# Mixture-of-experts stage: token rows turned by DMA instead of TensorE, weights in a ring of three slots addressed by registers

## The reference

```python
x = x + ga * attn(layernorm(x) * (1 + ca) + sa)        # 16 batches of 512 tokens, width 256
h = layernorm(x) * (1 + cb) + sb
normed = layernorm(h) * rn_g + rn_b
top_w, top_idx = top_k(normed @ router_w.T + router_b, 2)   # softmax over the two
for e in range(8):
    t = layernorm(h) * ln_g[e] + ln_b[e]
    t = gelu(t @ w1[e] + b1[e]) @ w2[e] + b2[e]         # 256 -> 1024 -> 256
    out += combine[e] * t                               # zero unless e is one of the token's two
x = x + gb * out
```

## Time and profile before

| | |
|---|---|
| median of 3 runs | 1253.28 us (1248.76 to 1253.87) |
| the profiled execution | 1263.39 us, span 1261.6 us |
| TensorE busy | 1123.1 us (89%) |
| VectorE busy | 912.2 us (72%) |
| ScalarE busy | 554.1 us (44%) |
| GpSimd busy | 588.1 us (47%) |
| granted TensorE clock, mean | 0.909 |

### The profile page before, as it was taken

How to read it: one execution, slowest core, us unless ns; L and a number is a source line. 1 busy time by engine, 2 the same in 40 slices (tenths; PEclk the granted TensorE clock), 3 DMA queues, 4 the chain that set the end, 5 groups by cost and what they waited for, 6 DMA issues and landing times.

```text
span 1261.6 us, 29766 instructions
## 1 busy us (share of the span) xinstructions
PE 1123.1 (89%) x8408; PEld 892.3 (71%) x8408; DVE 912.2 (72%) x2923; ACT 554.1 (44%) x1098; POOL 588.1 (47%) x487
## 2 busy tenths in 40 slices
PE   5789799889884329999999999999999999999996
PEld 1334454554443318998999999998999999998995
DVE  5577878877886426777777777777777777777775
ACT  1567565666563203433444444433434444433442
POOL 2111554554556572455554454445554444445553
PEclk8788878877796558999999999999999999999998
DMA  5346546556454265877444747457444444445743
GB/s 159 126 155 210 175 154 230 194 179 229 153 179 141 75 217 166 213 208 179 87 84 85 215 90 213 85 128 176 88 84 86 85 85 82 85 87 116 192 83 45
DMA packets 105765, 177.38 MB, mean 141 GB/s; under 512 B 23580, under 2 KB 76968, under 8 KB 99592
## 3 DMA queue, kind: packets, MB, share of 16 engines
q1 hardware_dynamic: 71560, 120.34, 30.7%
q0 software_dynamic: 34176, 56.72, 23.2%
HBM read 228.66 MB, written 63.69 MB: 232 GB/s over the span
## 4 chain that ended last, share of the span: by engine, by line
PE 71%; DVE 9%; issue 4%; POOL 3%; DMA 2%; another core or an unknown queue 1%; ACT 1%; DVEq 1%; POOLq 0%; SPq 0%; ACTq 0%
PE banks L1227 29%; PE banks L1215 29%; PE banks L1180 3%; PE banks L1204 3%; PE banks L1189 3%; DVE st L670 2%; POOL lists L461 2%; DMA lists<-nrm,slot 2%; PE banks L1101 2%; PE banks L1118 2%; DVE rowbuf L788 1%; DVE rowbuf L790 1%; DVE mv L675 1%; DVE resid L844 1%
## 5 line engine op out<-in xcount | busy, mean ns | idle before, releaser
L1215 PE MATMUL banks<-nh,wbuf 128*128 128x256 bf16 x2272 | 467.9, 274 | 9.8 <-ACT gf L641 8.3
L1227 PE MATMUL banks<-wbuf,resid 128*128 128x256 bf16 x3408 | 465.7, 273 | 0.0
L641 ACT ACTIVATE gf<-banks,b1t 128x256 f32<-128x256 f32 x568 | 269.3, 474 | 428.3 <-PE banks L1215 348.8
L497 POOL DMA_INDIRECT out<-rowbuf,ydst x142 | 232.0, 1634 | 353.2 <-DVE rowbuf L1008 279.5
L1227 PEld LDWEIGHTS banks<-wbuf,resid 128*128 128x128 bf16 x3408 | 334.1, 98 | 39.2
L1215 PE MATMUL banks<-nl,wbuf 128*128 128x256 bf16 x1136 | 311.1, 274 | 0.0
L1016 DVE CAST resid<-gf 128x256 bf16<-128x256 f32 x568 | 180.0, 317 | 178.6 <-ACT gf L641 110.9
L1018 DVE TENSOR_TENSOR resid<-gf,resid 128x256 bf16<-128x256 f32 x568 | 241.9, 426 | 19.5
L1215 PEld LDWEIGHTS banks<-nh,wbuf 128*128 128x128 bf16 x2272 | 223.2, 98 | 37.4 <-ACT gf L641 9.7
L461 POOL DMA_INDIRECT lists<-nrm,slot x128 | 138.4, 1081 | 142.2 <-DVE nrm L904 107.6
L488 POOL DMA_INDIRECT resid<-y_rows,ygb x142 | 145.3, 1023 | 54.9 <-issue 43.7
(11 more groups left out here) (184 smaller groups left out, 1101.5 us busy)
## 6 DMA issues: line engine op xcount, KB each, us to landing
wbuf<-wsplit SPq DMA_DIRECT2D x142, 1024.0 KB
rowbuf<-lists SPq DMA_DIRECT2D x71, 264.0 KB
wbuf<-in_L_ffn_w SPq DMA_DIRECT2D x16, 1024.0 KB, 6.7
wsplit<-wbuf SPq DMA_DIRECT2D x16, 1024.0 KB, 5.3
b2t<-in_L_ffn_b SPq DMA_DIRECT2D x71, 128.0 KB
resid<-in_L_attn_x SPq DMA_DIRECT2D x16, 512.0 KB, 7.4
out<-resid SPq DMA_DIRECT2D x16, 512.0 KB
csB<-mod_rows SPq DMA_DIRECT2D x16, 256.0 KB
```

Source lines behind the costliest of these rows:

```text
L497: g.indirect_dma_start(out_rows, bass.IndirectOffsetOnAxis(ap=ydst[:, r, h:h + 1], axis=0), yt[:, r, h, :], None, compute_op=ALU.add).then ...
L641: a.activation(gf[:, c % 2, :], MM[c % 2][:, 0:TOK], ACT.Gelu, bias=b1t[:, r, c:c + 1]).then_inc(gf_s, 1)
L1215: last = t.matmul(MM[c % 2][:, 0:TOK], w, m[:, r, k, :], start=n == 0, stop=n == 5)
L1227: last = t.matmul(ACC[r][h][:, 0:D], g[:, c, h * P:(h + 1) * P], w, start=c == 0 and n == 0, stop=c == NI - 1 and n == 2)
```

## The change

- The transposes of `turn` are gone from TensorE. ScalarE now copies the rows as bf16 straight from `xin` into `xhl`, VectorE writes the rest beside it, and SyncE turns both with two DMA transposes of 128x512 bf16 for a tile (`flip`) into `nhl`. ScalarE and VectorE do this two tiles ahead at chunk 5, SyncE a tile ahead.
- The weights lie in a ring of three slots (`wring`; the third lies over the last batches of `store`, the former `resid`). The two first experts are loaded before the table exists; from then on, when a tile is the first of expert e, expert e + 2 is loaded into the slot that is free (`weights_ahead`). Before, each expert was loaded into both buffers.
- The slot is a number in the table. TensorE reads the slots for two tiles with one load of three registers (`sets_from`), and its matmuls take the address of the weights from a register.
- The biases are now loaded on a condition too. SyncE reads six table entries for a tile, not three.
- VectorE keeps the token numbers in `ytok`, one small copy more for a tile, and builds four more rows of the table.

```diff
@@ SyncE
+            for e in range(2):
+                sp.dma_start(wbuf[:, e, 0:4096], wsplit_d[e, :, 0:4096]).then_inc(got_p1[e], 16)
+                sp.dma_start(wbuf[:, e, 4096:8192], wsplit_d[e, :, 4096:8192]).then_inc(got_p2[e], 16)
...
-                wait_past(sp, tr_s, j - 1)
-                wait_past(sp, yt_to, j - 1)
+                wait_past(sp, nl_s, j - 1)
+                wait_past(sp, yw_s, j - 1)
...
+            def entry(j, row, top):
+                return nc.sync.value_load(table[0:1, row, ds(j, 1)], min_val=0, max_val=top)
+            def weights_ahead(j, r):
+                e, new, s = entry(j, 5, E - 1), entry(j, 4, 1), entry(j, 6, 2)
+                sp.wait_ge(mm1_s, NI * j + 1)
+                sp.dma_start(wring[:, ds(s, 1), 0:4096], wsplit_d[ds(e, 1), :, 0:4096], cond=new).then_inc(got_w1[r], 16)
+                sp.wait_ge(mm2_s, NI * j + 1)
+                sp.dma_start(wring[:, ds(s, 1), 4096:8192], wsplit_d[ds(e, 1), :, 4096:8192], cond=new).then_inc(got_w2[r], 16)
+            def bias_load(j, r):
+                e, new = entry(j, 0, E - 1), entry(j, 2, 1)
...
+            def flip(j, r):
+                sp.wait_ge(nl_s, j + 1)
+                hold(sp, "sp")
+                wait_past(sp, mm1_s, NI * (j - 1))
+                hold(sp, "sp")
+                for h in range(TH):
+                    sp.dma_start_transpose(nhl[:, r, :, h * P:(h + 1) * P], xhl[:, r, h, :]).then_inc(got_nT[r], 16)
             def tile_loads(j, r):
-                rows_load(j, r)
-                e, new = which(j)
-                first_load(j, r, e, new)
-                second_load(j, r, e, new)
+                if not isinstance(j, int) or j + 1 < TILES:
+                    rows_load(j + 1, 1 - r)
+                flip(j, r)
+                bias_load(j, r)
+                if not isinstance(j, int) or j + 1 < TILES:
+                    weights_ahead(j - 1, 1 - r)
...
+            rows_load(1, 1)
+            bias_load(0, 0)
+            flip(0, 0)
+            sp.wait_ge(x2_out, 16 * NB)
@@ ScalarE
-                act.wait_ge(tr_s, j + 1)
-                wait_past(act, mm1_s, NI * (j - 1))
-                a.activation(nh[:, r, :, :].rearrange("p k n -> p (k n)"), TR[r][:, :], ACT.Copy).then_inc(nh_s, 1)
+                act.wait_ge(got_xin[r], 16 * half + 16)
+                wait_past(act, got_nT[r], 16 * TH * half)
+                hold(act, "act")
+                a.activation(xhl[:, r, :, 0:D], xin[:, r, :, 0:D], ACT.Copy).then_inc(nh_s, 1)
@@ TensorE
-            def turn(j, half, r):
...
+            def sets_from(j, n):
+                loads[0] += 1
+                in_reg = [t.alloc_register(f"slot{loads[0]}_{m}") for m in range(n)]
+                t.reg_load(in_reg, table[0:1, 3, ds(j, n)])
+                return [ds(t.snap(reg, donate=True, min_val=0, max_val=2), 1) for reg in in_reg]
...
-                    head = wbuf[:, r, k * I + c * P:k * I + (c + 1) * P]
+                    head = wring[:, s, k * I + c * P:k * I + (c + 1) * P]
...
             with t.Fori(1, (TILES - 1) // 2 - 1) as h:
-                tile(2 * h + 1, h, 1, False, False)
-                tile(2 * h + 2, h + 1, 0, False, False)
+                used_sets = sets_from(2 * h, 3)
+                tile(2 * h + 1, h, 1, False, used_sets[0], used_sets[1])
+                tile(2 * h + 2, h + 1, 0, False, used_sets[1], used_sets[2])
```

More of the change, by code:

```diff
@@ L1024, in tile @@
                         targets(j, half, r)
[L1025 to L1026 removed]
+                    if c == 5 and not (isinstance(j, int) and j + 2 >= TILES):
+                        split_rows(j + 2, half + 1, r)
                     if c == 6 and not last_tile:
@@ L1030, in _ @@
             dve.wait_ge(x2_out, 16 * NB)
-            split_rows(0, 0, 0)
+            for r in range(2):
+                split_rows(r, 0, r)
             destinations(0, 0, 0)
@@ L1195, in _, with first @@
             t.transpose(V[:, 0:E * NI], vrow[0:E * NI, :], ident[0:E * NI, 0:E * NI]).then_inc(b1v_ps, 1)
-            def turn(j, half, r):
-                pe.wait_ge(got_xin[r], 16 * half + 16)
-                wait_past(pe, nl_s, j - 1)
-                for k in range(NK):
-                    for h in range(TH):
-                        last = t.transpose(TR[r][:, k * TOK + h * P:k * TOK + (h + 1) * P], xin[:, r, h, k * P:(k + 1) * P], ident[:, :])
-                last.then_inc(tr_s, 1)
-            def first(j, r, c):
+            loads = [0]
+            def sets_from(j, n):
[3 more added lines that the diff above has]
+                return [ds(t.snap(reg, donate=True, min_val=0, max_val=2), 1) for reg in in_reg]
+            def first(j, r, s, c):
                 wait_past(pe, gf_s, NI * j + c - 1)
@@ L1230, in second, with tile @@
                 last.then_inc(mm2_s, 1)
-            def tile(j, half, r, is_first, is_last):
-                pe.wait_ge(nl_s, j + 1)
-                pe.wait_ge(got_w1[r], 16 * half + 16)
+            def tile(j, half, r, is_first, past, now):
+                pe.wait_ge(got_nT[r], 16 * TH * half + 16 * TH)
+                if isinstance(j, int) and j < 2:
+                    pe.wait_ge(got_p1[j], 16)
+                else:
+                    pe.wait_ge(got_w1[r], 16 * half)
+                hold(pe, "pe")
@@ L1235, in tile @@
                 for c in range(NI):
-                    first(j, r, c)
+                    first(j, r, now, c)
                     if c >= LAG:
                         if c == LAG:
-                            pe.wait_ge(got_w2[r], 16 * half + 16)
+                            if isinstance(j, int) and j < 2:
+                                pe.wait_ge(got_p2[j], 16)
+                            else:
+                                pe.wait_ge(got_w2[r], 16 * half)
                             wait_past(pe, yb_s, j - 1)
-                        second(j, r, c - LAG)
+                            hold(pe, "pe")
+                        second(j, r, now, c - LAG)
@@ L1242, in tile @@
                     elif not is_first:
-                        second(j - 1, 1 - r, NI - LAG + c)
-                    if c == 4 and not is_last:
-                        turn(j + 1, half + r, 1 - r)
-            turn(0, 0, 0)
+                        second(j - 1, 1 - r, past, NI - LAG + c)
+            pe.wait_ge(tab_s, 1)
+            hold(pe, "pe")
+            used_sets = sets_from(0, 3)
             for j in range(3):
-                tile(j, j // 2, j % 2, j == 0, False)
+                tile(j, j // 2, j % 2, j == 0, used_sets[j - 1], used_sets[j])
```

102 lines of the change are left out of this document (54 added, 48 removed).

## The result

The changed kernel takes 1244.01 us (median of 10, 1241.51 to 1247.58), the kernel before 1252.3 us (1248.76 to 1256.13). The ratio is 0.9934, 95% interval 0.9921 to 0.9947: 8.3 us faster, where 22 were forecast. The profiled execution after has a span of 1242.8 us.

A forecast was written before the change was run, and what follows sets the result against it. The prediction took TensorE's list to bound the expert stage. Its terms -30.8 + 5 + 3.5 made -22.3 us, which taken off the median of 1253.28 us gave 1231 us, range 1214 to 1266.

The forecast's parts named there:

- transposes, 70 x 0.44: TensorE's steady stretch: 70 groups of four transposes, 0.44 us each, would go, saving 30.8 us.
- loop heads: TensorE at each of 33 rounds: branch and table load would cost 0.15 us a round, 5 us.
- start: Before the first expert matmul: two DMA issues and a landing would add 1.7 to 4.2 us, taken as 3.5.
- rows behind the weights: SyncE's queue: rows, needed some 7 us after issue, would follow 2 MB of weights once per expert at no cost.
- That delays rows and transposes by some microseconds that this lead holds.: SyncE's queue: the delay by 2 MB of weights per expert would fit within the rows' lead of some 7 us.
- The nearest rival: TensorE's lead is too short at times; 10 to 28 us of gain go, giving 1236 to 1258 us; chance 0.15.
- TensorE's list: In the expert stage TensorE's list sets the time; 96 matmuls a tile take 10.47 us and the sequencer stays ahead.
- The rival of TensorE's sequencer: Matmuls with register addresses issue too slowly, beyond 44 ns a pair; at 55 ns about 1296 us; chance 0.11.
- SyncE: SyncE's list for a tile: 6.2 us plus two transposes at 1.2 makes 8.6 us, under TensorE's 10.47.
- The slower rival: SyncE's `tile_loads` becomes the bound; at 2.5 us a transpose about 1274 us, at 2.8 us 1316; chance 0.15.
- The -8 to +14 us put on what follows: Uncertainty, in both directions, for the stretch after the first expert matmul, up to the first steady transposes.
- The base: The sum was made against a 1263.39 us execution, 10.1 us above the median, then taken off the 1253.28 us median.

The follow-up runs named there:

- the second profile of before: The kernel before the change, unchanged, profiled once more: 1252.25 us, with a span of 1250.5 us.

## Why the prediction was wrong

Terms of the sum, forecast and measured (after against the second profile of before, both with rows at 455.7):

| term | forecast | measured |
|---|---|---|
| transposes, 70 x 0.44 | -30.8 | -30.6 (0.437 a tile: from 10.917 on average to 10.48 without a loop head) |
| loop heads | +5 | +3.3 |
| start | +3.5 | +6.2 (461.15 to 467.38) |
| rows behind the weights | 0 | +13.9 (11.3 of holes, 2.6 at the lower clock) |
| left over | | -0.5 (-0.6 of it in the first chunks behind the start) |
| sum | -22.3 | -7.7 |

- **The step that failed** is "That delays rows and transposes by some microseconds that this lead holds." The lead was nearly right (6.2 us, from 509.91 to where ScalarE begins to wait, 519.80 - 3.74). The landing was not worked out: the 2 MB take 8.9 us here (507.97 to 2.9 before 519.80; in the trace their packets move from 509.0 to 516.6 and the rows' from 515.8 to 518.6), and the rows come after them. The prediction took the row load's 2.8 us of the earlier trace rows, where nothing lay ahead. What it overlooked besides is who waits: ScalarE's copy stands at chunk 5 in front of GELUs. Leaving the loads out gave 1231.27 us, the very number forecast, which is no merit of the forecast (start and loop heads were also off, and nearly cancel) but shows that this one term was missing.
- **The nearest rival** was the first, part of the gain given back on TensorE, with 1236 to 1258 us. It had the place ("a GELU delayed by ScalarE's copy or at the loop's head") and the number, but not the cause: nothing is given back in an ordinary tile beyond 0.1 us a round, all of it follows five loads of weights.
- **TensorE's list**: right. The loop head costs 0.1 us a round and not 0.15, though its table load takes 0.77 us by the median and not 0.27. The table load was dearer than taken, and the sequencer's lead was longer than summed. The Trainium skill's floor of about 600 ns for a table load ("DMA: Bandwidth & Descriptors", latency and other measured facts) is near TensorE's 539 to 1029 ns, whose least value is below it, and does not fit SyncE's 261 at least. The consequence worked out from it, 0.45 us a head, did not come.
- **The rival of TensorE's sequencer** is out. The register operations of `first` from 1018.2 to 1019.1 us span a whole chunk:

```profile
L1250 PEldq FUSED_REGOPS  x5: 46/46/60, 1018.2 to 1019.1; - x5
```

  Twelve pairs and 6 register operations take 0.9 us. At 0.1 us for each of the latter, 0.3 us are left for 12 pairs, 25 ns each, and 44 was the limit. With the 62 ns of the Trainium skill ("TensorE: Matmul & The Clock Gate", part 1) 12 matmuls alone would take 0.74 us, so register addresses do not bring these into that case.
- **SyncE**: a transpose's issue was taken as 1.2 us and takes 1.28. The list was taken as 8.6 us and is 9.6. It is not the bound in the steady stretch, but it has no strength to make up for a delay; on the third chip, where its sequencer stands now and then, the kernel's gain shrank by 0.4%, some 5 us. The slower rival was thus nearer than it looked: one table load more, and on that chip the kernel is 1.7% slower than before.
- **The start**: the landing of the transposes (5.3 us from their issue, 4.9 by the median of all) is longer than the 2.8 taken from a plain load, and two biases go out ahead of them. The -8 to +14 us put on what follows came out at -0.6: the first chunks run closer together than in the second profile of before.
- **The base**: the sum was taken off the median although it was made against an execution 10 us slower. The second profile of the kernel before shows that this was right to do, since none of its terms lay in those 10 us.

## What to carry to other kernels

What is asked for right behind a bulk load must be costed at the bytes that are still ahead of it, not at its own landing time, and then the one who waits for it must be looked up in its engine's order. Moving the bulk only changes who is late. Here it helped to ask for it several microseconds before the small transfers and from an engine other than the one with the long list; a queue of its own did not let the small ones pass. An issuing engine with 90% of the tile in its list was no bound in one trace and cost time in another of the same kernel.

## What the hardware did unexpectedly

- A small load waits for bulk in another hardware queue about as long as for bulk in its own: its first packet moved 2.5 to 3.7 us after the issue with 102 to 121 packets of 8 KB not yet begun in queue 10, and 3.2 to 3.9 us with 96 to 109 of them in the same queue 1. The Trainium skill ("DMA: Bandwidth & Descriptors", issuing engines are not separate DMA queues) says that starting DMAs from several engines "will only save the time on the sequencer it takes to initiate the DMA". These packets agree; that the kernel with loads by ScalarE is 15.6 us faster does not speak against it, since the loads were also asked for at another time and SyncE's list was shorter.
- From GpSimd's software queue the same loads held the transposes up for 20 us (518.49 to 538.4). Their packets took turns with the weights', and both were slow; why, no run tells.
- A table load of three registers takes TensorE 0.77 us, one of one register SyncE 0.27.
- The same kernel in a sitting on another chip: simple instructions of SyncE's sequencer took up to 705 ns in place of 29, and the ratio to before went from 0.9934 to 0.9976.
